# Gates stored behind the rows for the experts and gathered with them; link tables made by VectorE and ScalarE

## The reference

```python
# graph layer: enh = layernorm(x) + 0.1 * query_emb
Q, K, V = enh @ Wq + bq, enh @ Wk + bk, enh @ Wv + bv      # 3125 x 4 heads x 64
scores = einsum(Q[dst], K[src] + 0.2 * rel[edge_type]) / 8
w      = softmax of scores over the edges of one dst
msgs   = segment_sum(w * V[src], dst)                      # V where a node has no edge
x      = x + layernorm(msgs @ Wo + bo + node) * gamma + beta
# experts: z = layernorm(x)
probs  = softmax(z @ gate_w + gate_b); the two largest, divided by their sum, are the gates
x      = x + sum over the two experts e of gate_e * (silu(z @ w1[e]) * (z @ w2[e])) @ w3[e]
```

## Time and profile before

| | us |
|---|---|
| median of 3 runs | 1187.59 |
| lowest, highest | 1181.28, 1190.45 |
| the profiled execution | 1183.72 |
| its span | 1182.0 |

### The profile page before, as it was taken

The page is one execution under the profiler, slowest core; times in us unless marked ns, Lnnn a source line. Parts: engine busy times, 40 slices in busy tenths (PEclk is TensorE's granted clock), DMA queues, the critical chain, the costliest instruction groups (busy, mean ns, idle before and its releaser), DMA issues.

```text
span 1182.0 us, 23559 instructions
## 1 busy us (share of the span) xinstructions
PE 1003.4 (85%) x7010; PEld 808.8 (68%) x7011; DVE 896.6 (76%) x1770; ACT 659.2 (56%) x2360; POOL 804.7 (68%) x777
## 2 busy tenths in 40 slices
PE   5988777888788888877887789958999999999994
PEld 2445455666566666655665666836999999999993
DVE  5868999999999999999999879994444444444441
ACT  3833478898998899888988756751111111111110
POOL 3648777777777777777777276505678786677773
PEclk8998988998999899999999989668999999999997
DMA  7345888888788888888788800374626427553322
GB/s 201 130 133 192 258 257 267 263 260 258 251 268 255 266 263 264 263 260 268 247 264 248 267 16 19 126 236 115 152 46 154 104 46 207 146 137 58 46 47 27
DMA packets 115039, 215.26 MB, mean 182 GB/s; under 512 B 21451, under 2 KB 59259, under 8 KB 114939
## 3 DMA queue, kind: packets, MB, share of 16 engines
q0 software_dynamic: 49536, 132.19, 39.2%
q1 hardware_dynamic: 63723, 80.57, 21.4%
q10 hardware_dynamic: 1680, 1.31, 0.4%
HBM read 191.47 MB, written 22.54 MB: 181 GB/s over the span
## 4 chain that ended last, share of the span: by engine, by line
PE 40%; DVE 23%; issue 16%; POOL 11%; DMA 5%; ACT 4%; DVEq 2%; SPq 0%; POOLq 0%; ACTq 0%
PE qe_ps L1847 14%; POOL ring L606 9%; PE bank L1856 8%; DVE ring L864 6%; PE bank L1847 4%; DVE acc L876 3%; DVE ring L858 3%; ACT wv L1444 3%; DMA out<-y_st,slot_i 2%; PE bank L1702 2%; PE qe_ps L1590 2%; PE qe_ps L1766 2%; DMA ring<-kv_table,src_idx 1%; PE qe_ps L1662 1%; DVE score L870 1%
## 5 line engine op out<-in xcount | busy, mean ns | idle before, releaser
L606 POOL DMA_INDIRECT ring<-kv_table,src_idx x440 | 427.7, 972 | 138.1 <-issue 123.2
L1444 ACT ACTIVATE wv<-ring,wgt 128x64 f32<-128x64 f32 x1628 | 406.1, 339 | 1.2 <-PE bank L1702 0.8
L1662 PE MATMUL qe_ps<-q,hot_t 128*128 x1320 | 200.1, 290 | 99.2 <-DVE ring L864 97.7
L1662 PEld LDWEIGHTS qe_ps<-q,hot_t 128*128 128x128 bf16 x1320 | 120.5, 102 | 151.6 <-issue 128.1
L1559 ACT ACTIVATE act<-qe_ps 128x512 f32<-128x512 f32 x64 | 38.2, 597 | 296.1 <-PE bank L1847 150.3
L1847 PEld LDWEIGHTS qe_ps<-xg_t,ring 128*128 128x128 f32 x1536 | 182.8, 193 | 4.9 <-ACT xg_t L1554 1.0
L1847 PE MATMUL qe_ps<-xg_t,ring 128*128 128x128 f32 x1536 | 183.4, 276 | 1.3 <-ACT xg_t L1554 0.7
L1702 PE MATMUL bank<-wv,hotf 128*128 128x260 f32 x588 | 164.6, 409 | 7.0 <-DVE acc L876 7.0
L680 POOL DMA_INDIRECT out<-y_st,slot_i x64 | 119.3, 1864 | 66.2 <-DMA out<-y_st,slot_i 33.2
L864 DVE TENSOR_TENSOR ring<-ring,qe_ps 128x512 f32<-128x512 f32 x220 | 148.4, 675 | 0.4 <-PE qe_ps L1662 0.3
L858 DVE TENSOR_TENSOR ring<-ring,bank 128x1024 f32<-128x1024 f32 x110 | 133.1, 1210 | 5.3 <-DMA ring<-kv_table,src_idx 5.0
(11 more groups left out here) (334 smaller groups left out, 1590.9 us busy)
## 6 DMA issues: line engine op xcount, KB each, us to landing
ring<-in_w SPq DMA_DIRECT2D x48, 512.0 KB, 5.5
d_row<-d_rows SPq DMA_DIRECT2D x55, 256.0 KB, 5.5
t_row<-t_rows SPq DMA_DIRECT2D x55, 256.0 KB
ring<-kv_table,src_idx POOLq DMA_INDIRECT x440, 4.3
kv_table<-ring SPq DMA_DIRECT2D x25, 256.0 KB, 2.0
out<-acc SPq DMA_DIRECT2D x26, 128.0 KB, 1.7
x_table<-ring SPq DMA_DIRECT2D x26, 128.0 KB, 1.9
ring<-in_x SPq DMA_DIRECT2D x12, 256.0 KB, 9.5
```

Of the source, the lines that this page charges most:

```text
L606: pool.indirect_dma_start(ring[:, u, place(g) * D:(place(g) + 2) * D], None, kv_table, bass.IndirectOffsetOnAxis(ap=src_idx[:, 4 * g + u:4 ...
L1444: ins = act.activation(wv[:, g % WV_N, u, h, 0:HD], v_rows(g)[:, u, h * HD:(h + 1) * HD], ACT.Copy, scale=w[:, col:col + 1])
L1662: ins = pe.matmul(q_ps[p % AHEAD][:, u * D:(u + 1) * D], hot_t[:, p // 4 % HB_N, hot_cols(p, u)], tile_of(q3, q_tiles[p % 4])[:, k * D:(k ...
```

## The change

**Link tables.** `links()` is gone from POOL. `link_f` is one row of flags, one longer than the steps, so that the flag of the next step is a shifted view of it. POOL clears its ends in its first part. DVE makes the two products for `hop_f` itself before it sets `ends`. The scaling is folded in ACT's activations (`BIG * x` and a bias), three of them, issued after the middle piece of query tile 4 and before the high piece of tile 5; `odd_row` takes in the constant by one more operation on DVE.

**Gates.** `gate_table` and its gathers are gone. A row of `x3_table` is 272 values long: 256 of the token and its 16 gates. SP's row stores write the first 256, the store of `cm` (same place in SP's order) writes the last 16, in pieces of 64 bytes as before. `gather_x` brings both, so it now waits for that store, and for DVE's pick of the gates from the buffer that it overwrites. The gates' small operations on DVE move ahead of the ranks of the last tiles; the two large products that make `cm` move to POOL. In the experts' loop DVE multiplies the 16 gates of a row by a one-hot row of the block's expert (`block_hot`, made from `beq`, which is now also the memory of POOL's products) and reduces them to one.

```diff
+ROW = D + NX
...
-        x3_table = dram("x3_table", (NP, D))
-        gate_table = dram("gate_table", (NP * NX, 1))
+        x3_table = dram("x3_table", (NP, ROW))
...
-            def links():
-                event("ends").wait(pool)
-                pool.memset(hop_f[:, :, STEPS:], 0.0)
-                pool.memset(link_f[:, :, STEPS:], 0.0)
-                pool.memset(link_f[:, 0, 0:1], 0.0)
-                c(pool.memset(link_f[:, 1, STEPS - 1:STEPS], 0.0))
-                c(pool.tensor_copy(link_f[:, 1, 0:STEPS - 1], link_f[:, 0, 1:STEPS]))
-                c(pool.tensor_tensor(hop_f[:, 1, 0:STEPS], hop_f[:, 0, 0:STEPS], link_f[:, 1, 0:STEPS], ALU.mult))
-                c(pool.tensor_tensor(hop_f[:, 0, 0:STEPS], hop_f[:, 0, 0:STEPS], link_f[:, 0, 0:STEPS], ALU.mult))
-                c(pool.tensor_scalar(hop[:, :, :], hop_f[:, :, :], -1.0, BIG, ALU.add, ALU.mult))
-                c(pool.tensor_scalar(link_f[:, :, :], link_f[:, :, :], -1.0, BIG, ALU.add, ALU.mult))
-
-                for i in range(2):
-                    c(pool.tensor_scalar(link[:, i, :], link_f[:, i, :], odd_row[:, i + 1:i + 2], None, ALU.add))
-                event("diffs").set(pool)
...
             gather(DEPTH - 1)
-            links()
             for g in range(DEPTH, QUADS):
                 gather(g)
...
-            event("no_gates").set(pool)
+
+            event("gate_pairs").wait(pool)
+            c(pool.tensor_tensor(gate_parts[:, :, :, :], oh[:, :, :, :], gates[:, :, :].unsqueeze(3).to_broadcast([P, NODE_TILES, 2, NX]), ALU.mult))
+            c(pool.tensor_tensor(cm[:, 0:NODE_TILES, :], gate_parts[:, :, 0, :], gate_parts[:, :, 1, :], ALU.add))
+            event("gates").set(pool)
             event("slots").wait(pool)
             pool.wait_ge(s_x3, 16 * NT)
+            pool.wait_ge(s_gt, 16)
 
             def gather_x(b):
                 f_tx.wait(pool, b - XB)
+                f_gp.wait(pool, b - XB)
                 pool.indirect_dma_start(xg[:, b % XB, :], None, x3_table, bass.IndirectOffsetOnAxis(ap=slot_i[:, b:b + 1], axis=0)).then_inc(s_xg[b % XB], 16)
...
-            for b in range(3):
-                gather_x(b)
-            event("gate_rows").wait(pool)
-            pool.wait_ge(s_gt, 16)
-            for b in range(GATES):
-                gather_gates(b)
-            for b in range(3, XB - 1):
+            for b in range(XB - 1):
                 gather_x(b)
...
-                if b + GATES < BLOCKS:
-                    gather_gates(b + GATES)
...
-            c(v.tensor_copy(hop_f[:, 1, 0:STEPS], bank[1][:, 0:STEPS]))
-            v.tensor_tensor(link_f[:, 0, 1:STEPS], d_first[:, 1:STEPS], hop_f[:, 1, 0:STEPS - 1], ALU.is_equal)
-            c(v.tensor_tensor(hop_f[:, 0, 0:STEPS], d_first, hop_f[:, 1, 0:STEPS], ALU.is_equal))
+            c(v.tensor_copy(d_last, bank[1][:, 0:STEPS]))
+            event("consts").wait(v)
+            v.tensor_tensor(link_f[:, 1:STEPS], d_first[:, 1:], d_last[:, 0:STEPS - 1], ALU.is_equal)
+            c(v.tensor_tensor(one_node, d_first, d_last, ALU.is_equal))
+
+            for i in range(2):
+                ins = v.tensor_tensor(hop_f[:, i, 0:STEPS], one_node, link_f[:, i:i + STEPS], ALU.mult)
+            c(ins)
             event("ends").set(v)
...
+            c(v.tensor_tensor(gates[:, :, 1], top[:, :, 1], top[:, :, 0], ALU.subtract))
+            event("dl").set(v)
             place_tokens(0)
             ranks(0)
             place_tokens(1)
+            event("dexp").wait(v)
+            c(v.tensor_scalar(gates[:, :, 0], gates[:, :, 1], 1.0, None, ALU.add))
+            c(v.reciprocal(gates[:, :, 0], gates[:, :, 0]))
+            c(v.tensor_tensor(gates[:, :, 1], gates[:, :, 1], gates[:, :, 0], ALU.mult))
+            event("gate_pairs").set(v)
...
+            v.tensor_tensor(block_hot[:, :, 1:], beq[:, :, 0:NX - 1], beq[:, :, 1:], ALU.subtract)
+            c(v.tensor_scalar(block_hot[:, :, 0], beq[:, :, 0], -1.0, 1.0, ALU.mult, ALU.add))
+
+            def gates_of(b):
+                v.wait_ge(s_xg[b % XB], 16 * (b // XB + 1))
+                f_gs.wait(v, b - 2)
+                v.tensor_tensor(gate_pick[:, b % 2, :], xg[:, b % XB, D:ROW], block_hot[:, b, :], ALU.mult).then_inc(f_gp.sem, 1)
+
+            def gate_of(b):
+                f_gp.wait(v, b)
+                v.tensor_reduce(gate_s[:, b:b + 1], gate_pick[:, b % 2, :], AX.X, ALU.add).then_inc(f_gs.sem, 1)
...
             for b in range(1, BLOCKS):
                 if b + 1 < BLOCKS:
                     copy_weights(b + 1)
+                gates_of(b)
                 gated(b)
+                gate_of(b)
                 take_y(b - 1)
...
-            sp.dma_start(gate_table.rearrange("(t p x) a -> p t (x a)", p=P, x=NX), cm[:, :, :]).then_inc(s_gt, 16)
+            sp.dma_start(x3_table[:, D:ROW].rearrange("(t p) x -> p t x", p=P), cm[:, :, :]).then_inc(s_gt, 16)
...
+            def steps_links():
+                event("consts").wait(act)
+                event("ends").wait(act)
+                act.activation(hop[:, :, :], hop_f[:, :, :], ACT.Identity, bias=run[:, 0:1], scale=BIG)
+
+                for i in range(2):
+                    ins = act.activation(link[:, i, :], link_f[:, i:i + CHUNKS * CS], ACT.Identity, bias=odd_row[:, i + 1:i + 2], scale=BIG)
+                ins.then_inc(event("diffs").sem, 1)
+
```

More of the change, by code:

```diff
@@ L273, in build @@
         tmp_s = carve(acc_flat, 3 * STEPS).rearrange("p (i s) -> p i s", i=3)
-        d_first = tmp_s[:, 1, :]
+        d_last, d_first, one_node = (tmp_s[:, i, :] for i in range(3))
         both_i = carve(acc_flat, 2 * STEPS, I32).rearrange("p (i s) -> p i s", i=2)
@@ L407, in build @@
         slot_f = sb("slot_f", [P, BLOCKS])
-        gate_i = sb("gate_i", [P, BLOCKS], I32)
-        gate_st = sb("gate_st", [P, GB, 1])
+        gate_parts = beq[:, :, :].rearrange("p b x -> p (b x)")[:, 0:NODE_TILES * 2 * NX].rearrange("p (t k x) -> p t k x", k=2, x=NX)
+        block_hot = sb("block_hot", [P, BLOCKS, NX], BF16)
+        gate_pick = sb("gate_pick", [P, 2, NX])
+        gate_s = sb("gate_s", [P, BLOCKS])
         row_at = sb("row_at", [P, 2])
@@ L473, in build @@
         s_ys = [sem(f"s_ys{i}") for i in range(YB)]
-        s_gr = [sem(f"s_gr{i}") for i in range(GB)]
+        f_gp, f_gs = Count(sem("f_gp")), Count(sem("f_gs"))
         s_gt = sem("s_gt")
@@ L1198, in _ @@
             sb_ = [P, BLOCKS, NX]
+            event("gates").wait(v)
             c(v.tensor_tensor(beq[:, :, :], x_inc.unsqueeze(1).to_broadcast(sb_), iota_row[:, 0:BLOCKS].unsqueeze(2).to_broadcast(sb_), ALU.is_le))
@@ L1217, in _ @@
             copy_weights(0)
-            c(v.tensor_scalar(bef[:, :], bef[:, :], float(NX - 1), None, ALU.min))
-            c(v.scalar_tensor_tensor(out=gate_i[:, :], in0=slot_f[:, :], scalar=float(NX), in1=bef[:, :], op0=ALU.mult, op1=ALU.add))
-            event("gate_rows").set(v)
             copy_weights(1)
+            v.tensor_tensor(block_hot[:, :, 1:], beq[:, :, 0:NX - 1], beq[:, :, 1:], ALU.subtract)
[7 more added lines that the diff above has]
+                v.tensor_reduce(gate_s[:, b:b + 1], gate_pick[:, b % 2, :], AX.X, ALU.add).then_inc(f_gs.sem, 1)
             def gated(b):
@@ L1229, in take_y @@
                 f_y.wait(v, b)
-                v.wait_ge(s_gr[b % GB], 16 * (b // GB + 1))
+                f_gs.wait(v, b)
                 if b >= YB:
                     v.wait_ge(s_ys[b % YB], 16 * (b // YB))
-                v.tensor_scalar(y_st[:, b % YB, :], bank[6 + b % 2][:, 0:D], gate_st[:, b % GB, :], None, ALU.mult).then_inc(f_yc.sem, 1)
+                v.tensor_scalar(y_st[:, b % YB, :], bank[6 + b % 2][:, 0:D], gate_s[:, b:b + 1], None, ALU.mult).then_inc(f_yc.sem, 1)
+            gates_of(0)
             gated(0)
+            gate_of(0)
             for b in range(1, BLOCKS):
@@ L1419, in _ @@
                     high_piece(i)
-                if i >= 1:
+                if i >= 1 and i != Q_FIRST:
                     middle_piece(i - 1)
+                if i == Q_FIRST - 1:
+                    middle_piece(i)
+                    steps_links()
                 if i == NODE_TILES - 5:
```

31 lines of the change are left out of this document (10 added, 21 removed).

## The result

The kernel after takes 1179.81 us (median of 20 runs, 1174.66 to 1190.56); before, on the same chip, 1187.69 (20 runs, 1181.28 to 1195.11). The ratio is 0.9956, 95% interval 0.9935 to 0.9977: 5.2 us faster (2.7 to 7.7); the two medians lie 7.9 apart. The forecast was 4.7 us faster. Its parts fared less well than its sum.

What follows compares the result with a forecast made beforehand. DVE or POOL was taken to bound the edge loop, PE the experts' loop, then POOL's scatter chain. Terms 0.9 - 2.5 + 6.3 = 4.7 us off gave 1179.0 against the profiled execution, 1182.9 against the median; range 1176 to 1191.

Steps and rivals of the forecast that it cites:

- The tail: End of experts' loop: without gate gathers the late scatters catch up, last scatter 6.3 us sooner, bounds 0 and 6.5.
- Rival A: Experts' loop: scatters and DVE's weight copies stay locked in phase, tail gives 0, 1189.2 us; chance 0.17.
- The start of the experts' loop: Before the first blocks: first row gather waits for the gates' store; cost 2.5 us, bounds 1.1 and 8.2.
- The slots' part: DVE before the experts' loop: slots come 1.6 us later, at 802.8 instead of 801.2.
- rival C: Start of experts' loop: gates' store lands late, first gather 7 us later, 1188.6 us; chance 0.1.
- The step behind it: First row gather to PE's start: gather 3.0 us later but issued faster; 2.0 to 3.0 arrive, 2.5 taken.
- The edge loop: Link tables' sum for the edge loop: 1.4 + 0.7 - 1.2 = +0.9 us, bounds -1.2 and +6.4.
- The two products: DVE ahead of "ends": two hop_f products of 440 columns, costing 1.2 us on the path.
- the gathers' 1.4 us: Edge loop: POOL's earlier gathers save 1.4 of DVE's 5.0 us of waits for gathers, bounds 0 and 5.0.
- The port: Early edge loop: DVE products no longer slowed by POOL's operations; 0.7 of 2.6 us arrives, bounds 0 and 2.6.
- Rival B: Early edge loop: all 2.6 us of DVE's slowed products come back, 6.6 us gained, 1181.0; chance 0.13.
- D: Rival, edge loop: POOL's head start reaches DVE whole, 10.2 us gained, 1177.4; chance 0.08.

Runs made afterwards that it cites:

- e4: The kernel after plus a gather of 4 bytes a row behind each row gather, for which y waits; 1421.68 us, 1.0038 of before.
- e12: Before with the gates part alone, gates' store issued behind the first expert's load, 30 idle PE products instead of 20; 1377.74 us, 0.9909 of before.
- e13: After with the gates' store behind the first expert's load, hop_f products in DVE's idle time, 30 idle PE products instead of 20; 1385.76 us, 0.9972 of before.
- e10: After with the gates' store issued behind the first expert's load and the hop_f products moved into DVE's idle time; 1382.48 us, 0.9993 of before.
- e9: Before with the gates part alone, link tables left on POOL, second run; 1380.35 us, 0.9970 of before.
- e0: The kernel after, unchanged but for one DVE register instruction, on another chip; 1416.17 us, 1.0001 of before.

## Why the prediction was right, point by point

**The tail: +6.3, measured +6.36.** Right in mechanism and size: scatter 62 goes behind its own y, the last one 4.49 us later. "One block's round against one block's time" was the right way to see it, and e4 shows it from the other side. The rate was less sure than the forecast has it. Behind the end of y the scatters of before and after are 14.1 and 9.5 us late at block 43, 9.9 and 3.3 at block 57; in between a round takes 5.21 and 5.07 us in the mean, not 5.5 and 4.4. So 4.6 of after's lead of 6.6 us were there by block 43, and rounds of 4.4 us in a row come only from block 57 on, when POOL has issued its last row gather. The full 6.3 needed some luck, as e12 and e13 show. What was left out is the stretch behind the last scatter, 2.56 us in the two profiles; two profiles of kernels that differ in POOL's stream would have shown it.

**Rival A, 0.17.** It did not decide in after, but it wasn't wrong: e13 and before show the lock in phase, and what sets it off, a y that waits for its buffer. The forecast named the lock but not what sets it off, and took the lag itself for harmless. After passed that point, block 38, with 10.2 us of lag, against 11.1 to 12.2 in e12, e13 and before.

**The start of the experts' loop: -2.5, measured -2.67** (the stretches from the first store of rows to turn_x(0), -1.52 and -1.15). The slots' part was put at 1.6, measured 1.52; the store landed 3.9 us after its issue (4.0 taken), which rules out rival C. (No row shows the 1.7 us of clock in C's sum; block 0 took 1.4 to 3.0 us more at a lower clock than at 1.00.) The step behind it was right too in after: a late gather is issued in 0.99 us, an early one in 1.94, so of 2.4 us only 1.15 arrive. But the forecast stopped at turn_x(0). Block 0 takes 3.8 to 6.8 us by PE's clock, a spread larger than the whole term; that it cost only 0.2 between these two profiles is chance. The first gather itself moved by 3.9 us (1.52 and 2.41), not by 3.0.

**The edge loop: +0.9, measured -0.99. This step failed.** The two products cost what was said (first column of the table: 1.1 in the mean; 1.6 in this pair). PE's wait of 1.30 us fell to 0.64, the 0.7 taken. POOL has no tensor operation between gathers any more, and its head start went as foretold, in waits for reduces:

```profile
106.15 0.94 POOL L610 DMA_INDIRECT ring<-kv_table,src_idx  x1 [1.94 <-DVE score L856]
113.44 0.95 POOL L610 DMA_INDIRECT ring<-kv_table,src_idx  x1 [2.58 <-DVE score L856]
121.09 0.95 POOL L610 DMA_INDIRECT ring<-kv_table,src_idx  x1 [2.94 <-DVE score L856]
...
POOL ring L610 <- DVE score L856: 18.9, 18, 3.0
DVE ring L844 <- DMA ring<-kv_table,src_idx: 5.9, 10, 0.9
```

The last two lines are waits from 100 to 800 us. The term that was mis-sized is the gathers' 1.4 us: DVE's waits for gathers were to fall from 5.0 to 3.6, and are 5.9. Up to 200 us they did fall, from 3.6 to 2.3, nearly the 1.4. Measured from the first gather, DVE's add of quad 20 came as in before (124.76 and 124.75), so the 1.7 us that after was late at quad 0 were won back by then. The last 1.0 went behind that, between quads 60 and 80, in waits for gathers (3.6 us after 200 us, 1.3 in before), where POOL and DVE run at one pace and no edit was made; the forecast had let the waits stay there. Whether that second loss is the change's or the transfers' timing of one execution is open: the other chips are too unsteady for it. Their times only say that the tables' part brings no gain there.

**The port: 0.7 of 2.6.** The two pairs of products that took 1.90 and 2.17 us now take 0.75 us, and 0.42 and 0.43 one by one, but in their place DVE waits for ACT:

```profile
103.06 0.42 DVE L725 TENSOR_TENSOR wv<-bank,q 128x256 f32<-128x256 f32 x1 [0.59 <-ACT q L1383]
104.33 0.42 DVE L725 TENSOR_TENSOR wv<-qe_ps,q 128x256 f32<-128x256 f32 x1 [0.85 <-ACT q L1383]
106.40 0.75 DVE L729 TENSOR_TENSOR q<-wv,q 128x256 bf16<-128x256 f32 x2
110.26 0.43 DVE L729 TENSOR_TENSOR q<-wv,q 128x256 bf16<-128x256 f32 x1 [1.46 <-ACT q L1387]
```

Rival B, all 2.6 back, is out, and D with it. By the rule of the Trainium skill (SBUF — State Buffer, "SBUF: two separate sides") on the exclusive lock the whole 2.6 us would have come back to DVE. The trace agrees with the lock, in the 0.75; but no run shows 2.6 us gained, and the time went to the next in line. That 0.7 arrived is worked out from PE's wait alone.

**The sum.** 4.7 forecast, 5.2 measured, 3.2 between the two profiles. It held by luck in part: a loss not seen (1.9 in the edge loop's term) met a gain not seen (2.56 behind the last scatter). The first 1.55 us, to the first gather, are none of the change's: it goes at 83.67, 81.25 and 82.68 us in three profiles of after, at 82.12 and 82.25 in two of before.

## What to carry to other kernels

Where a chain of transfers ends a kernel, compare its round with the time of one step of the loop: an instruction of 1.25 us, in a queue that was busy for 15 of 20 us, was worth some 6 to 9 us at the end, because with it the round was so near the step that delays were hardly won back. Leave a margin: without it two of nine profiles still ended with late scatters. Before issuing something earlier, follow the gain to the engine that sets the time: its clock after a gap took back all of it in e10, and a semaphore that it opens late took back part of it in e12. And test the halves of a change apart: one half carried the gain, the other brought none that could be measured.

## What the runs showed of the hardware

**Short casts of VectorE were held by a product of GpSimd.** In after DVE's ranks run beside POOL's products of 800 and 400 columns (783.91 to 785.46, 785.54 to 786.59):

```profile
784.06 1.43 DVE L1140 CAST xrow_i<-xrow 128x16 int32<-128x16 f32 x1
785.52 0.18 DVE L1141 TENSOR_SCALAR xrow_i<-xrow_i 128x16 int32<-128x16 int32 x1
785.73 0.90 DVE L1142 CAST xrow<-xrow_i 128x16 f32<-128x16 int32 x1
```

Each cast of 16 columns has one input and takes 0.17 us elsewhere; here both end within 0.04 us of POOL's product, after 1.43 and 0.90 us, and so they do in all profiles with the gates part. The operation with a scalar between them took 0.18, but it says nothing: it starts between the two products, 0.02 us ahead of the second. The forecast had put 2 us on operations with two inputs; the two casts lost 2.0 us, so that size was right by luck. The section of the Trainium skill named above counts casts, with copies and operations with a scalar, among the operations of VectorE that can enter the 2-port modes and then contend with GpSimd. The trace agrees for these casts between fp32 and int32.

**PE's clock after a short gap.** After 0.62, 1.26 and 2.02 us of idle time behind the idle products 32 products took 3.81 us, at a granted clock of 1.00 (2.4 GHz); in the eleven profiles with 2.47 to 3.94 us of idle time they took 5.2 to 6.8, at 0.56 to 0.78 where it was read. Ten idle products more were enough in both kernels that had them. One of the three fast cases, e9, had 20 like the slow ones, so where between 2.02 and 2.47 us the difference lies, or whether it is the same each time, isn't shown.

**PE can stop without a wait.** On three chips of four PE stood in the edge loop while it waited for nothing that the profile shows ("issue"): some 175 us from 100 to 800 us in e0, and nothing of it in the experts' loop. Why is not shown.
